# Identity transposes on TensorE between the rounds of eight layer norms of a four-layer graph network

## The reference, cut to what matters

```python
def _layernorm(x, axis=-1, eps=1e-05):
    m = jnp.mean(x, axis=axis, keepdims=True)
    v = jnp.var(x, axis=axis, keepdims=True)
    return (x - m) / jnp.sqrt(v + eps)
...
    x = x + _L0_gnn_ref(_layernorm(x, axis=-1), adj, ...)
    x = x + _L0_ffn_ref(_layernorm(x, axis=-1), ...)
...
```

## Time and profile before

| | us |
|---|---|
| median of 3 runs | 3227.18 |
| lowest and highest | 3210.18, 3233.53 |
| the profiled execution, its own time | 3232.81 |
| its span, from the first to the last instruction | 3231.1 |

### The profile page before, as it was taken

The page is one execution under the profiler, slowest core; times in us unless marked ns, Lnnn a source line. Parts: engine busy times, 40 slices in busy tenths (PEclk is TensorE's granted clock), DMA queues, the critical chain, the costliest instruction groups (busy, mean ns, idle before and its releaser), DMA issues. The chain is left out here.

```text
span 3231.1 us, 50387 instructions
## 1 busy us (share of the span) xinstructions
PE 2550.3 (79%) x18894; PEld 1622.8 (50%) x18894; DVE 2118.4 (66%) x4172; ACT 1312.0 (41%) x2383; POOL 733.6 (23%) x766
## 2 busy tenths in 40 slices
PE   6467999999999999995567577868749989986840
PEld 5433555555555555553426465634426666652740
DVE  5836787777788778866566797666743457856111
ACT  4323444444444444442336403323214445543630
POOL 0000000000000000011007581067710033410766
PEclk7678999999999999997768857679879979886975
DMA  4311222222222221222123412000012211102332
GB/s 78 110 34 33 50 54 57 56 57 55 51 51 50 51 51 51 50 52 85 50 65 90 77 43 29 7 11 6 6 33 65 62 44 42 45 7 66 98 82 72
DMA packets 177585, 167.48 MB, mean 52 GB/s; under 512 B 82532, under 2 KB 150512, under 8 KB 174664
## 3 DMA queue, kind: packets, MB, share of 16 engines
q1 hardware_dynamic: 156368, 131.86, 16.3%
q0 software_dynamic: 20992, 32.59, 4.8%
HBM read 131.35 MB, written 33.02 MB: 51 GB/s over the span
## 5 line engine op out<-in xcount | busy, mean ns | idle before, releaser
L2995 PE MATMUL hy_ps<-hy_uT,hy_win 128*128 128x512 f32 x1152 | 500.3, 595 | 0.0
L2995 PEld LDWEIGHTS hy_ps<-hy_uT,hy_win 128*128 128x128 f32 x1152 | 218.4, 191 | 283.6 <-issue 272.0
L1913 POOL DMA_DIRECT2D ek_w<-ek_src x32 | 18.0, 561 | 1168.6 <-DVE ek_dst L1935 1168.6
L3057 PE MATMUL hy_ps<-hy_wo,hy_yg 128*128 128x512 f32 x512 | 238.0, 609 | 10.2 <-ACT XNP L3197 8.7
L1184 POOL DMA_INDIRECT f_xg<-f_xn,f_gidx x188 | 178.5, 949 | 112.3 <-POOLq L971 55.2
L1198 POOL DMA_INDIRECT XNP<-f_y,f_pidx x160 | 172.0, 1075 | 79.7 <-issue 48.1
L2498 PE MATMUL er_c<-XNG 128*128 128x400 f32 x480 | 180.9, 533 | 0.0
L3057 PEld LDWEIGHTS hy_ps<-hy_wo,hy_yg 128*128 128x128 f32 x512 | 93.6, 192 | 120.1 <-issue 98.2
L3276 DVE TENSOR_TENSOR_SCAN XNG<-XNG,hy_fx 128x2048 f32<-128x2048 f32 x32 | 141.6, 4425 | 2.9 <-issue 0.4
L1290 DVE TENSOR_TENSOR f_ysl<-f_py,f_cur 128x256 f32<-128x256 f32 x94 | 39.8, 424 | 143.1 <-PE f_py L1225 142.6
L2431 POOL DMA_INDIRECT er_gone<-er_nodes,er_sidx x120 | 123.8, 1031 | 36.6 <-issue 34.7
(11 more groups left out here) (666 smaller groups left out, 6002.1 us busy)
## 6 DMA issues: line engine op xcount, KB each, us to landing
XNG<-hy_decays SPq DMA_DIRECT2D x32, 1024.0 KB, 10.7
hy_rb<-hy_inverse SPq DMA_DIRECT2D x128, 128.0 KB, 3.4
f_y<-f_ysl SPq DMA_DIRECT2D x94, 128.0 KB, 2.0
f_gb<-gate_rows SPq DMA_DIRECT2D x16, 640.0 KB, 5.1
g_KB<-g_keys SPq DMA_DIRECT2D x32, 320.0 KB, 4.3
f_xn<-XNG SPq DMA_DIRECT2D x4, 1280.0 KB, 6.0
hy_xn<-XNP SPq DMA_DIRECT2D x1, 4096.0 KB, 12.9
hy_XC<-hy_xn SPq DMA_DIRECT2D x16, 256.0 KB, 3.8
```

What stands on the lines that cost most here:

```text
L2995: mm = pe.matmul(p[:], win[:, t, m * 128:(m + 1) * 128], uT[:, t, :], start=(t == 0), stop=(t == KT - 1))
L3057: mm = pe.matmul(PS[4 + q % 2][:], yg[:, t, q * 128:(q + 1) * 128], wo[:, t, :], start=(t == 0), stop=(t == KT - 1))
```

## The change

`layer_norm` gets a helper that transposes the identity matrix n times into the first part of `pin[0]`. It is called in each round behind `back(o)`, ahead of the late part of the round: two transposes with `slots`, four without; in the ninth turn of the loop eight. Where `pin` has been in use, TensorE waits once for the tenth copy ahead of the loop. Nobody reads the results, and no semaphore counts them.

```diff
+            def busy(n):
+                for _ in range(n):
+                    pe.transpose(pin[0][:, 0, :], g.ident[:], g.ident[:])
+
+            if turned:
+                pe.wait_ge(copied, GI)
             for o in range(GO + 1):
                 if o < GO:
                     back(o)
+                    busy(2 if slots else 4)
+                else:
+                    busy(8)
                 if slots and o >= 1:
                     turn(2 * o - 2)
                     turn(2 * o - 1)
```

## The result

| | before | after |
|---|---|---|
| median | 3225.53 (6 runs) | 3252.53 (6 runs) |
| lowest and highest | 3210.18, 3235.59 | 3243.63, 3256.7 |
| the profiled execution, its own time | 3232.81 | 3248.72 |
| its span | 3231.1 | 3247.0 |

The ratio, after to before, is 1.0068, with an interval of 1.004 to 1.0095: slower by 22 us by the ratio, by 27 us by the medians. The forecast was +15 us, with a chance of 0.72 for +8 to +25: the 22 us lie in that, the 27 just outside, and both lie in the range of 3222 to 3264. The profiled executions lie 15.9 us apart.

A forecast was written before the change was run, and what follows sets the result against it. No engine was taken to bound the kernel throughout (TensorE busy 79%, VectorE 66%); stages follow one another, so norm growth moves everything behind. Terms 5 + 11.4 - 1.5 = +15 us on 3227.2 gave 3242 us, range 3222 to 3264.

The forecast's parts named there:

- Price of one identity transpose: On TensorE, 0.11 us at the high clock and 0.214 at the low one; all 256 exposed cost 28 or 55 us.
- The slots norms: n0, n2, n5, n7: rounds grow from 1.58 to 1.65 us; +1.25 us each, 5 us in all.
- The logits norms: n3, n6, n8: six rounds longer by 0.44 us plus delays at both ends; +3.8 us each, 11.4 in all.
- the end that has all 40 exposed: Upper end for the three logits norms: all 40 transposes exposed at 0.11 us each, 13 us in all.
- the 0.7 us of rounds 0 and 1: Start of a logits norm: nine low-clock transposes per round, projections then at high clock; round 2 begins 0.7 us late.
- n1, 0, and -1.5 behind it: n1 costs 0, at most 0.5 us; weight transposes behind it gain up to 3 us from the clock, half counted.
- Other places where the clock could carry over: Mainly the adjacency stage behind n0, running at the low clock: 5 us at stake, counted as 0, the end being -5.
- The rule against it: Skill's rule that transposes don't engage the full rate: nothing carries over and n1's 1.5 us go; the trace disagreed.
- That the identity doesn't keep the clock up: Rival, in the norms: clock rises later, every added transpose costs its low-clock price, 55 us, 3282 us; chance 0.08.
- That the waits take them in: Rival: waits absorb the transposes and the clock carries over behind n0 and n1; -8 us, 3219 us; chance 0.14.
- That the change does nothing: Rival: unread transposes leave no trace or fit a free slot of TensorE's queue; 3227 us; chance 0.06.

The follow-up runs named there:

- again: The kernel before, built and run again with nothing changed; ratio 1.0017 to the kernel before.
- logits_only: The kernel before with the change's identity transposes in n3, n6 and n8 alone, 120 of the 256; ratio 1.0018 to the kernel before.
- n1_only: The kernel before with the change's identity transposes in n1 alone, 40 of the 256; ratio 1.0026 to the kernel before.
- after_again: The changed kernel run once more as it is; ratio 1.0078 to the kernel before.
- slots_only: The kernel before with the change's identity transposes in n0, n2, n5 and n7 alone, 96 of the 256; ratio 1.0005 to the kernel before.
- iota_before: The kernel before with GpSimd's iota moved ahead of the edge keys' write-back, its wait and the next load; ratio 0.9983 to the kernel before.
- best: The kernel before with identity transposes in waits ahead of round 0 (four behind it except n1), 128 ahead of l0_ffn, and GpSimd's iota moved; ratio 0.9956, 3220.48 us.
- after_shift: The changed kernel with 64 more identity transposes ahead of round 0 of n0, 128 in all ahead of l0_ffn; ratio 1.0041 to the kernel before.
- iota_after: The changed kernel with GpSimd's iota moved ahead of the edge keys' write-back, its wait and the next load; ratio 1.0025 to the kernel before.

## Why the prediction was right, and where it fell short

The direction, the verdict and the range held. That the ratio's 22 us fall within +8 to +25, though 10 to 13 of them come from a loop that nobody had in the sum, is owed to the width of that range. By its steps:

- **Price of one identity transpose.** 0.11 us at the high clock and 0.215 at the low one, as worked out.
- **The slots norms, +1.25 each, 5 in all.** Over the four kernels without them (before, again, logits_only, n1_only) the mean is 17.2, over the three with them (after, after_again, slots_only) 18.4: 1.1 each, 4.5 in all. The round came at 1.63 for a predicted 1.65.
- **The logits norms, +3.8 each, 11.4 in all.** In the same way from 19.4 to 23.8: 4.35 each, 13.1 in all, near the end that has all 40 exposed (4.4 each). The term that was too small is the 0.7 us of rounds 0 and 1. The projections start at 1635.86, 4.03 us behind round 0 (1631.83), for a predicted 3.84. And the high clock was to come before them, with 0.27 us each: the four take 1.76 us, the first three starting 0.5 apart. So round 2 begins 5.72 us behind round 0, where it was 4.60: 1.1 us late.
- **n1, 0, and -1.5 behind it.** The norm is 0.5 us shorter. Of the stage behind it half of the three microseconds was counted as kept. All of it is: from the first weight transpose to the next stage it was 160.92 - 147.06 = 13.86 us, now 155.22 - 144.22 = 11.00. 0.5 of it is lost again ahead of it, to the eight unread transposes of the ninth turn. They were to end before ScalarE's last copy and end behind it, at 143.12 and 142.56. Net -2.4, if it is the change's at all: in `slots_only` and `iota_before`, with nothing added in n1 (in `iota_before` nowhere), n1 takes 12.26 us as well and the first 36 weight loads behind it 3.91. In all nine profiles with transposes in n1 the clock was up there, in two of the five without. The loads in before, after and `iota_before`:

```profile
147.06 6.79 PEld L2776 LDWEIGHTS hy_ps<-ident,hy_raw_in 128*128 128x128 f32 x36 [2.25 <-issue]
144.22 3.92 PEld L2785 LDWEIGHTS hy_ps<-ident,hy_raw_in 128*128 128x128 f32 x36 [1.35 <-issue]
144.63 3.91 PEld L2781 LDWEIGHTS hy_ps<-ident,hy_raw_in 128*128 128x128 f32 x36 [2.09 <-issue]
```

- **Other places where the clock could carry over, 0 with the end -5.** Behind n0 the first 16 weight loads of the adjacency take 1.96 us where they took 3.48, and eight of them take 1.13 us, the pace of the high clock, from 70.34 on, where that came after 75; the stretch from the end of n0 to the first L368 of n1 is 3 us shorter in after and in after_again (67.7 and 67.8 for 71.1). It is not in `slots_only`, where n0 has the same transposes (72.2), and `iota_before`, with none, has half of it (69.3). So this hangs on more than the change and was rightly not counted on, though it did come.
- **The rule against it**, that of the Trainium skill ("TensorE: Matmul & The Clock Gate", Part 4) that the full rate "doesn't engage for transpose-mode". It does not hold here for float32: in `best` identity transposes alone raise the clock from 0.50 to 1.00 and hold it.
- **The rivals.** That the identity doesn't keep the clock up falls with the norms' clock of 0.86 to 0.89. That the waits take them in falls with the round of n3, 2.31 us; the high clock that this rival had behind n0 and n1 did come. That the change does nothing falls with 256 rows of L287.

**The step that failed is the one that carried only the norms and the stages next to them into the sum, and everything else at 0.** The meeting of the engines ends what the data of a stage hand on, but not what its instructions do: 64 added transposes ahead of l0_ffn moved the fetches in a loop that starts 24 us behind n1, and that cost 10 to 13 us there. With it the sum is 17 (norms) + 10 to 13 (l0_ffn; the stage behind n1 lies in it) - 3 (behind n0) = 24 to 27, for a measured 22 to 27. `after_shift` is the control: the same change without the moved fetches is at 1.0041, which is 13 us, the forecast's 15 less 2.

Some things stay open. The rest of after is 14 us shorter in its profile, of which 3 are the stage behind n0; parts behind n2, n5, n6 and n7 are 2 to 3 us shorter each, but again, which changes nothing, is 5 us shorter too. What makes the clock fall in single chunks of l0_ffn, which is where most of its 13 us lie, was not tried. And the stretch behind n7 takes between 287 and 305 us in kernels that don't differ there; no run was aimed at it. The carrier of what is left of l0_ffn's growth in iota_after is not shown.

## What to carry to other kernels

A wait can take in unread work only where it stands: look whether the idle time is ahead of a burst or between its rounds, and put the warming ahead, where it turned a loss of 17 us in the norms into a gain of 10. Added instructions on an engine can cost time in a later loop that they have nothing to do with; before a difference of half a per cent is put down to the change, run a control with the same number of instructions somewhere harmless, and the kernel itself again. Where a queue holds a cheap instruction that others need behind a wait for a transfer, it can be moved ahead: that took 9 us off the changed kernel's l0_ffn, though nothing measurable off the kernel before. And before a clock that stays up is booked as a change's gain, look at kernels without the change: here two of five had it too.

## What the runs showed of the hardware that had not been expected

- Instruction fetches, 16 KB packets on a queue of their own, fall at the same places in each pass of an unrolled loop here, where a pass has 1281 TensorE records and five fetches. Instructions on TensorE ahead of the loop shift the places; 128 float32 transposes bring them back. A write-back of 64 KB with a fetch that begins less than 2.1 us behind its issue takes 3.77 us in the mean until the next load, the others 3.24.
- Single falls of the granted clock make up most of what a long loop loses: each chunk of l0_ffn (from the third on) with a short stretch at 0.50 takes 80.5 to 82.3 us, every other one 78.5 to 79.9.
- Transposes of a float32 identity, with nothing else on TensorE, raise the clock from 0.50 to 1.00 and hold it (windows of `best`).
- The same kernel, built and run again, came out at 1.0017, 1.0001 to 1.0032, of itself.
